# Attention inner loop: two units' value products after four score pairs, instead of one unit's after two

## The chip, the cores and the metric

The kernel runs on one core of a Trainium2 chip. The metric is device microseconds of one execution, from start to end on that core; a kernel is timed in several executions and the median counts. All times below are microseconds (us) unless marked ns.

## What is computed

The reference is one transformer layer with the norm behind each half, for one sequence of 2048 tokens, width 256, 16 heads of 16 channels, in float32:

```python
Q = X @ Wq + bq;  K = X @ Wk + bk;  V = X @ Wv + bv         # 16 heads of 16
scores = einsum('bhqd,bhkd->bhqk', q, k) / sqrt(16)
out = einsum('bhqk,bhkd->bhqd', softmax(scores), v)
out = out.transpose(0, 3, 2, 1).reshape(b, s, 256)
x = layernorm(X + out @ Wo + bo)
ffn = qmatmul(silu(qmatmul(x, w_gate)) * qmatmul(x, w_up), w_down)   # int8 weights, width 1024
x = layernorm(x + ffn)
```

## The kernel before

The kernel has three stretches: the projections of Q, K and V (up to about 47 us, with loads of keys and queries behind), the attention loop (about 53 to 541 us), and the feed-forward part (to the end). The change is in the attention loop alone.

**Units.** The loop goes over 16 steps. A step is one chunk of 512 queries for one quad of four heads (`s = u // UPS`, `UPS` = 16). A step has 16 units, one for each tile of 128 keys, so there are 256 units. Unit `u` has four heads, handled as two *score pairs* of two heads each: pair `g = 2 * u + p`, 512 pairs in all.

**Four kinds of work per unit.**
- `scores(g)` (line 1041, TensorE): two matmuls, one per head, on the two halves of the array's rows (partitions 0 and 64 on). They fill two banks of PSUM, `ps[:, 2 * ring]` and the next, with `ring = g % 3`.
- the exponential (line 556, ScalarE): one instruction over 128x1024 elements reads both banks and writes `probs[:, u % 3, 2 * p : 2 * p + 2]`. So `probs` has three slots, one for each of three units.
- `prob_times_v(u)` (line 1057, TensorE; "the value product of unit u" below): four matmuls in float32, one per head, with 17 columns of weights each (16 channels and a column of ones that gives the softmax's denominator), on four column groups of the array. They accumulate over the 16 units of a step into one PSUM bank, `ACC`. The trace shows eight matmul records for the four.
- `save_attn` (line 711, VectorE): once a step, the accumulated bank is copied out. The next step's first value product waits for it (`attn_saved`, line 1054).

**What orders them.** Each engine runs its own list of instructions in order, and semaphores join them:

```python
pe.wait_ge(exp_done, g - 2)          # line 1038, before scores(g): pair g-3 has been read
pe.wait_ge(exp_done, 2 * (u + 1))    # line 1055, before prob_times_v(u)
if p == 0 and u >= 3:                # line 553, ScalarE, before the exponential of pair 2u
    act.wait_ge(pv_done, u - 2)      # line 555: value product u-3 done, its slot is free
```

The first protects the three pairs of PSUM banks. The last protects the three slots of `probs`: the first exponential of unit `u` overwrites what the value product of unit `u-3` reads. `prob_times_v` counts up `pv_done` once, with its last matmul.

**Guests of the loop.** For three chunks, TensorE also does the output projection of the chunk before (`project_out`, line 1081, twice, in units 4 and 7 of steps 5, 9 and 13) and the transposes behind the first norm (`turn_y`, line 1095, in units 4 and 7 of steps 6, 10 and 14). They stand behind the value products of their unit.

**Loads beside the loop.** SyncE issues the loads of keys, queries and the shift rows (lines 300 to 325) from one queue. The scores of a step's first unit wait for the queries and shift rows of that step (`q_loaded`, line 1024). The shift rows of step 1 are issued behind the keys of the last quad (line 385). From step 2 on, the loads are issued a step ahead.

Of the kernel before, what the change touches and what calls it, by code (L numbers as in the profile page):

```python
# [6 lines left out]
def layer_program(nc, X, Wq, bq, Wk, bk, Wv, bv, Wo, bo, w_gate, w_up, w_down, s_gate, s_up, s_down, out):  # L7
# [36 lines left out]
    with ExitStack() as ctx:  # L44
# [842 lines left out]
        def _(pe):  # L887
# [130 lines left out]
            def scores(g):  # L1018

                u, p = g // 2, g % 2  # L1020
                s, kt, ring = u // UPS, u % UPS, g % 3
                slot = s % NSLOT
                if kt == 0 and p == 0:
                    pe.wait_ge(q_loaded[slot], loaded(s))
                    if s < QUADS:
                        pe.wait_ge(k_loaded[s], keys_of(s))
                        pe.wait_ge(ones_ready, 2 * (s + 1))
                    if s < NSLOT:
                        pe.wait_ge(bound_ready, 2 * (s + 1))
                if g == 0:  # L1030

                    pe.wait_ge(norms_ready, 2)
                elif g < 3:

                    pe.wait_ge(v_ready, 2 * (g + 1))
                else:

                    pe.wait_ge(exp_done, g - 2)
                for half in range(2):
                    base = HALF * half  # L1040
                    last = nc.tensor.matmul(ps[:, 2 * ring + half, :],  # L1041
                                            k_stack[s % QUADS][base:base + ROWS, p, kt * P:(kt + 1) * P],
                                            q_slot[slot][base:base + ROWS, p, :], start=True, stop=True)
                last.then_inc(scores_ready, 1)

            def prob_times_v(u):

                s, kt = u // UPS, u % UPS
                if u == 0:
                    pe.wait_ge(v_ones, 1)  # L1050
                    pe.wait_ge(v_ready, TT // 2)
                elif kt == 0:

                    pe.wait_ge(attn_saved, s)
                pe.wait_ge(exp_done, 2 * (u + 1))
                for hh in range(NQ):
                    last = nc.tensor.matmul(ps[32 * hh:32 * hh + VW, ACC, :],  # L1057
                                            v_all[:, kt, NQ * (s % QUADS) + hh, :],
                                            probs[:, u % 3, hh, :], start=(kt == 0), stop=(kt == TT - 1))
                last.then_inc(pv_done, 1)  # L1060

            def project_out(c, b):

                bank = FFN_BANK if c < LAST else 6 + b
                if b == 0:
                    pe.wait_ge(attn_scaled, c + 1)
                if c == 0 and b == 0:
                    pe.wait_ge(w_loaded[3], 16)
                if b == 0 and c == LAST:

                    pe.wait_ge(down_free, 2)
                if b == 0 and c:

                    pe.wait_ge(yt_ready, KO * c)
                if b == 1 and c < LAST:

                    pe.wait_ge(ln1_sum, 2 * c + 1)
                for half in range(2):
                    j = 2 * b + half
                    for ko in range(KO):  # L1080
                        last = nc.tensor.matmul(ps[:, bank, half * HID:(half + 1) * HID],  # L1081
                                                at32[:, ko, CH * j:CH * (j + 1), :].rearrange("p d u -> p (d u)"),
                                                wo[:, ko, :], start=(ko == 0), stop=(ko == KO - 1))
                last.then_inc(wo_psum, 1)

            def turn_y(c, ko):

                bank = FFN_BANK if c < LAST else 6 + ko
                if ko == 0:
                    pe.wait_ge(ln1_ready, TPC * (c + 1))  # L1090
                elif c < LAST:

                    pe.wait_ge(yt_ready, KO * c + 1)
                for j in range(TPC):
                    last = nc.tensor.transpose(ps[:, bank, j * P:(j + 1) * P], x_by[:, j, c, ko * P:(ko + 1) * P],
                                               ident[:])
                last.then_inc(yt_psum, 1)
# [3 lines left out]
            for u in range(UNITS):  # L1101
                scores(2 * u)
                scores(2 * u + 1)
                if u >= 2:
                    prob_times_v(u - 2)
                s, kt = u // UPS, u % UPS
                c = s // QUADS - 1
                if c >= 0 and s % QUADS == 1 and kt in (4, 7):
                    project_out(c, kt // 7)
                if c >= 0 and s % QUADS == 2 and kt in (4, 7):  # L1110
                    turn_y(c, kt // 7)
# [71 lines left out]
```

## Time and profile before

| what | value |
|---|---|
| time, median of 3 runs | 660.39 us (659.87 to 661.35) |
| time of the profiled execution | 661.55 us |
| its span, first to last instruction | 659.8 us |
| mean granted TensorE clock | 0.974 |
| TensorE matmuls busy | 625.1 us (95%) |
| ScalarE busy | 533.1 us (81%) |
| VectorE busy | 158.6 us (24%) |
| GpSimd busy | 69.0 us (10%) |

The profile is that of one execution. Busy time of an engine is the union of its records. Ends of matmuls are modelled, and ScalarE's record of an instruction begins before the one ahead of it has ended, so neither engine's busy share alone tells which of them sets the pace. "PE" is TensorE's matmuls, "PEld" its weight loads, "ACT" ScalarE, "DVE" VectorE, "SPq" SyncE's issuing of DMAs. A row of the timeline merges neighbouring instructions of one group: x8 is eight of them.

### The profile page before, as it was taken

The numbers are of one execution on the slowest core, as the hardware profiler recorded it, in microseconds if no ns is written. First come the engines' busy times: TensorE is split into PE (matmuls) and PEld (weight loads), VectorE is DVE, ScalarE is ACT, GpSimd is POOL, SyncE is SP. The second block draws the span as 40 slices with busy tenths as digits, with TensorE's granted clock in tenths as the row PEclk, the third lists the DMA queues.
The fourth block names the chain that finished last, engine by engine and source line by source line (L and its number), as shares of the span: only waits on it lengthen the run. The fifth ranks groups of instructions, "written<-read, shape, count | busy, mean of one in ns | idle before, by whom it ended". The sixth has DMA issues, their size and how long they took to land.

```text
span 659.8 us, 9645 instructions
## 1 busy us (share of the span) xinstructions
PE 625.1 (95%) x3938; PEld 262.0 (40%) x3938; DVE 158.6 (24%) x280; ACT 533.1 (81%) x613; POOL 69.0 (10%) x53
## 2 busy tenths in 40 slices
PE   7997969999999999999999999999999997979994
PEld 6882212222222323222232322223322235958874
DVE  6684000000001201000021200001510004695684
ACT  4526969999999899999989999999999974233351
POOL 6658600000000000000000000000400000010001
PEclk9996979999999999999999999999999997999997
DMA  9577930101112010101210110111010001010111
GB/s 215 106 107 114 128 57 8 29 6 31 18 20 60 10 26 10 28 7 30 49 24 13 22 25 10 29 41 30 6 31 3 9 2 41 1 33 0 33 33 32
DMA packets 36032, 24.40 MB, mean 37 GB/s; under 512 B 24792, under 2 KB 30808, under 8 KB 35408
## 3 DMA queue, kind: packets, MB, share of 16 engines
q1 hardware_dynamic: 34302, 23.14, 20.3%
q10 hardware_dynamic: 1682, 0.60, 0.4%
q8 instruction: 33, 0.54, 0.3%
q14 instruction: 15, 0.12, 0.1%
HBM read 6.56 MB, written 4.33 MB: 17 GB/s over the span
## 4 chain that ended last, share of the span: by engine, by line
PE 82%; SPq 7%; DVE 6%; ACT 2%; issue 1%; ACTq 1%; DMA 1%; DVEq 0%
PE ps L1057 36%; PE ps L1041 30%; PE ps L1153 5%; PE ps L1132 5%; SPq L311 4%; PE ps L920 3%; PE ps L1081 2%; SPq L313 2%; DVE h L829 1%; DVE h_lo L817 1%; ACTq L565 1%; PE ps L906 1%; DMA x_tok<-in_L_attn_X 1%; DVE stats L793 1%; SPq L300 1%
## 5 line engine op out<-in xcount | busy, mean ns | idle before, releaser
L556 ACT ACTIVATE probs<-ps 128x1024 f32<-128x1024 f32 x512 | 470.5, 1386 | 32.4 <-PE ps L1041 32.4
L1057 PE MATMUL ps<-probs,v_all 128*17 128x512 f32 x2048 | 271.8, 603 | 0.6 <-ACT probs L556 0.4
L1041 PE MATMUL ps<-q_slot,k_stack 51*128 51x512 f32 x1024 | 228.7, 492 | 11.2 <-DMA q_slot<-shift 5.7
L1041 PEld LDWEIGHTS ps<-q_slot,k_stack 51*128 51x128 f32 x1024 | 94.1, 186 | 271.4 <-ACT probs L556 245.1
L711 DVE COPY attn_q<-ps 128x512 f32<-128x512 f32 x16 | 11.1, 692 | 376.2 <-PE ps L1057 376.2
L581 ACT ACTIVATE sg<-ps,sgate_c 128x512 f32<-128x512 f32 x32 | 21.9, 688 | 61.5 <-PE ps L1153 55.5
L1057 PEld LDWEIGHTS ps<-probs,v_all 128*17 128x17 f32 x2048 | 34.1, 95 | 70.2 <-issue 63.9
L475 POOL TENSOR_TENSOR rstd<-var_eps,minus_half 128x4 f32<-128x4 f32 x4 | 4.1, 1022 | 488.9 <-DVE var_eps L743 488.9
L1153 PE MATMUL ps<-qy,wg 128*128 128x512 f32 x128 | 38.5, 425 | 9.1 <-DVE h L829 9.0
L1153 PE MATMUL ps<-qy,wu 128*128 128x512 f32 x128 | 36.1, 406 | 0.0
L1153 PEld LDWEIGHTS ps<-qy,wg 128*128 128x128 f32 x128 | 24.0, 199 | 18.8 <-DVE h L829 13.4
L1132 PE MATMUL ps<-wd,h_hi 128*128 128x256 f32 x128 | 30.9, 283 | 0.0
L1132 PE MATMUL ps<-wd,h_lo 128*128 128x256 f32 x128 | 30.9, 283 | 0.0
L829 DVE SCALAR_TENSOR_TENSOR h<-ps,sup_c,sg 128x512 f32<-128x512 f32 x32 | 23.9, 748 | 23.6 <-ACT sg L581 23.3
L436 POOL MEMSET k_stack<- 3x4096 f32 x8 | 29.1, 3637 | 3.4 <-DMA k_stack<-k_part 2.8
L1153 PEld LDWEIGHTS ps<-qy,wu 128*128 128x128 f32 x128 | 25.3, 198 | 5.9
L1132 PEld LDWEIGHTS ps<-wd,h_hi 128*128 128x128 f32 x128 | 24.7, 193 | 0.2
L1132 PEld LDWEIGHTS ps<-wd,h_lo 128*128 128x128 f32 x128 | 24.6, 192 | 0.2
L574 ACT CAST h_hi<-h 128x512 fp32r<-128x512 f32 x32 | 19.6, 613 | 3.0 <-DVE h L829 3.0
L817 DVE TENSOR_TENSOR h_lo<-h,h_hi 128x512 fp32r<-128x512 f32 x32 | 21.9, 683 | 0.4
L1081 PE MATMUL ps<-wo,at 128*128 128x256 f32 x64 | 15.6, 389 | 0.0
L1081 PEld LDWEIGHTS ps<-wo,at 128*128 128x128 f32 x64 | 11.7, 189 | 6.5 <-issue 5.1
(88 smaller groups left out, 279.1 us busy)
## 6 DMA issues: line engine op xcount, KB each, us to landing
q_slot<-qy SPq DMA_DIRECT2D x64, 64.0 KB
k_stack<-k_part SPq DMA_DIRECT2D x12, 256.0 KB, 6.3
at<-at_dram SPq DMA_DIRECT2D x8, 272.0 KB, 2.8
at_dram<-attn_q SPq DMA_DIRECT2D x62, 34.0 KB
x_tok<-in_L_attn_X SPq DMA_DIRECT2D x16, 128.0 KB, 5.3
q_slot<-qy SPq DMA_DIRECT2D x64, 32.0 KB
k_stack<-k_part SPq DMA_DIRECT2D x12, 128.0 KB, 5.1
out<-out_tmp SPq DMA_DIRECT2D x12, 128.0 KB, 2.2
```

The source lines that it names most:

```text
L311: sp.dma_start(dst[base:base + 2 * HD, hh // 2, first:last], src[row:row + HD, 0:2, first:last]).then_inc(k_loaded[quad], 16)
L436: nc.gpsimd.memset(k_stack[quad].bitcast(f32)[HALF * half:HALF * half + PROD, :, :], 1.0).then_inc(ones_ready, 1)
L556: nc.scalar.activation(probs[:, u % 3, 2 * p:2 * p + 2, :].rearrange("p a b -> p (a b)"), ps[:, 2 * ring:2 * ring + 2, :].rearrange("p a b ...
L581: nc.scalar.activation(sg[:, u % 2, :], ps[:, u % 2, :], ACT.Silu, scale=sgate_c[:, u % MT:u % MT + 1]).then_inc(silu_done, 1)
L817: nc.vector.tensor_tensor(h_lo[:, u % MT, :], h32[:, u % 2, :], h_hi[:, u % MT, :].bitcast(f32), ALU.subtract).then_inc(h_ready, 1)
L829: nc.vector.scalar_tensor_tensor(h32[:, u % 2, :], ps[:, 2 + u % 2, :], sup_c[:, m:m + 1], sg[:, u % 2, :], ALU.mult, ALU.mult).then_inc(g ...
L920: last = nc.tensor.matmul(dst, w(ko), x(ko), start=(n == 0), stop=(n == len(terms) - 1))
L1041: last = nc.tensor.matmul(ps[:, 2 * ring + half, :], k_stack[s % QUADS][base:base + ROWS, p, kt * P:(kt + 1) * P], q_slot[slot][base:base ...
L1057: last = nc.tensor.matmul(ps[32 * hh:32 * hh + VW, ACC, :], v_all[:, kt, NQ * (s % QUADS) + hh, :], probs[:, u % 3, hh, :], start=(kt == 0 ...
L1081: last = nc.tensor.matmul(ps[:, bank, half * HID:(half + 1) * HID], at32[:, ko, CH * j:CH * (j + 1), :].rearrange("p d u -> p (d u)"), wo[ ...
L1132: last = nc.tensor.matmul(ps[:, 4 + i, 0:HID], h[:, m, i * P:(i + 1) * P], wd[:, m, :], start=(m == 0 and j == 0), stop=(m == MT - 1 and j ...
L1153: last = nc.tensor.matmul(ps[:, bank, :], w[:, ko, m * P:(m + 1) * P], qy[:, c, ko, part, :], start=(ko == 0 and part == 0), stop=(ko == K ...
```

## The change

The loop on TensorE runs the value products of two units in every second iteration. With `u` odd and at least 3, the order becomes scores of pairs 2u-2 and 2u-1 (the iteration before), scores of pairs 2u and 2u+1, then the value products of units u-3 and u-2. The last two value products, of units 254 and 255, stay behind the loop as before. No semaphore, wait count or buffer changes, and no other engine's list.

```diff
             for u in range(UNITS):
                 scores(2 * u)
                 scores(2 * u + 1)
-                if u >= 2:
+                if u >= 3 and u % 2:
+                    prob_times_v(u - 3)
                     prob_times_v(u - 2)
                 s, kt = u // UPS, u % UPS
                 c = s // QUADS - 1
                 if c >= 0 and s % QUADS == 1 and kt in (4, 7):
                     project_out(c, kt // 7)
                 if c >= 0 and s % QUADS == 2 and kt in (4, 7):
                     turn_y(c, kt // 7)
             prob_times_v(UNITS - 2)
             prob_times_v(UNITS - 1)
```

## Rows read from the trace of the kernel before

**Rows 1.** The page: span and busy time of each engine.

```profile
span 659.8 us, 9645 instructions
PE 625.1 (95%) x3938; PEld 262.0 (40%) x3938; DVE 158.6 (24%) x280; ACT 533.1 (81%) x613; POOL 69.0 (10%) x53
```

**Rows 2.** Groups by line, 150 to 500 us: busy, mean ns | idle before, releaser.

```profile
L556 ACT ACTIVATE probs<-ps 128x1024 f32<-128x1024 f32 x375 | 345.1, 1409 | 7.3 <-PE ps L1041 7.3
L1057 PE MATMUL ps<-probs,v_all 128*17 128x512 f32 x1496 | 196.8, 598 | 0.0
```

**Rows 3.** Timeline, 87 to 100 us: start, length, what [idle before, releaser].

```profile
89.48 1.22 PE L1041 MATMUL ps<-q_slot,k_stack 51*128 51x512 f32 x4 [5.72 <-DMA q_slot<-shift]
...
90.32 1.94 ACT L556 ACTIVATE probs<-ps 128x1024 f32<-128x1024 f32 x2 [5.34 <-PE ps L1041]
...
93.31 7.44 ACT L556 ACTIVATE probs<-ps 128x1024 f32<-128x1024 f32 x8 [1.05 <-PE ps L1041]
...
97.03 1.05 PE L1057 MATMUL ps<-probs,v_all 128*17 128x512 f32 x8
...
98.01 0.73 PE L1041 MATMUL ps<-q_slot,k_stack 51*128 51x512 f32 x4
...
98.68 1.05 PE L1057 MATMUL ps<-probs,v_all 128*17 128x512 f32 x8
```

**Rows 4.** Timeline of ScalarE alone around 318 us, three narrow looks.

```profile
316.25 2.56 ACT L556 ACTIVATE probs<-ps 128x1024 f32<-128x1024 f32 x2
...
317.15 2.58 ACT L556 ACTIVATE probs<-ps 128x1024 f32<-128x1024 f32 x2
...
318.98 1.67 ACT L556 ACTIVATE probs<-ps 128x1024 f32<-128x1024 f32 x1
```

**Rows 5.** Timeline of weight loads alone, 320 to 322 us.

```profile
320.28 0.19 PEld L1041 LDWEIGHTS ps<-q_slot,k_stack 51*128 51x128 f32 x2 [0.85 <-ACT probs L556]
320.70 0.19 PEld L1041 LDWEIGHTS ps<-q_slot,k_stack 51*128 51x128 f32 x2 [0.24 <-ACT probs L556]
321.14 0.13 PEld L1057 LDWEIGHTS ps<-probs,v_all 128*17 128x17 f32 x8 [0.25 <-issue]
```

**Rows 6.** Timeline, 300 to 308 us, with one copy by VectorE.

```profile
300.97 1.05 PE L1057 MATMUL ps<-probs,v_all 128*17 128x512 f32 x8
...
302.09 0.69 DVE L711 COPY attn_q<-ps 128x512 f32<-128x512 f32 x1 [28.65 <-PE ps L1057]
```

**Rows 7.** Timeline, 535 to 541 us: the end of the loop.

```profile
534.27 5.27 ACT L556 ACTIVATE probs<-ps 128x1024 f32<-128x1024 f32 x5
...
537.28 1.91 PE L1057 MATMUL ps<-probs,v_all 128*17 128x512 f32 x16
...
539.60 1.05 PE L1057 MATMUL ps<-probs,v_all 128*17 128x512 f32 x8 [0.41 <-ACT probs L556]
```

**Rows 8.** Timeline, 209 to 226 us: an output projection inside the loop.

```profile
216.80 1.99 PE L1081 MATMUL ps<-wo,at 128*128 128x256 f32 x8
218.72 0.30 PEld L1041 LDWEIGHTS ps<-q_slot,k_stack 51*128 51x128 f32 x4 [0.33 <-issue]
...
219.27 5.61 ACT L556 ACTIVATE probs<-ps 128x1024 f32<-128x1024 f32 x6 [1.19 <-PE ps L1041]
```

**Rows 9.** Timeline of TensorE alone, 250 to 261 us: transposes inside the loop.

```profile
254.31 0.65 PE L1095 MATMUL ps<-ident,x_tok 128*128 128x128 f32 x4
254.89 0.73 PE L1041 MATMUL ps<-q_slot,k_stack 51*128 51x512 f32 x4
```

**Rows 10.** Timeline, 52 to 64 us: the start of the loop.

```profile
53.78 5.61 ACT L556 ACTIVATE probs<-ps 128x1024 f32<-128x1024 f32 x6 [17.12 <-PE ps L1041]
...
56.69 0.29 PEld L1041 LDWEIGHTS ps<-q_slot,k_stack 51*128 51x128 f32 x2 [0.63 <-ACT probs L556]
...
57.41 1.91 PE L1057 MATMUL ps<-probs,v_all 128*17 128x512 f32 x8
...
62.23 0.39 PEld L1041 LDWEIGHTS ps<-q_slot,k_stack 51*128 51x128 f32 x4 [1.69 <-ACT probs L556]
...
62.87 1.94 ACT L556 ACTIVATE probs<-ps 128x1024 f32<-128x1024 f32 x2 [0.85 <-PE ps L1041]
```

**Rows 11.** Timeline, 62 to 92 us: the exponentials of step 0, and SyncE's shift loads.

```profile
61.01 1.02 ACT L556 ACTIVATE probs<-ps 128x1024 f32<-128x1024 f32 x1
...
62.87 22.11 ACT L556 ACTIVATE probs<-ps 128x1024 f32<-128x1024 f32 x24 [0.85 <-PE ps L1041]
...
85.80 2.54 SPq L325 DMA_DIRECT2D q_slot<-shift  x4
```

**Rows 12.** Busy time by stretch: PE, PEld, DVE, ACT, POOL, granted clock, DMA share, GB/s.

```profile
56.00:58.00 2.00, 1.88 (x8) 0.50 (x12) 0.29 (x1) 2.00 (x3) 0.00 (x0) 0.50 0.41 85
84.00:86.00 2.00, 0.00 (x0) 0.00 (x0) 0.00 (x0) 0.98 (x2) 0.00 (x0) 1.00 0.78 102
88.00:90.00 2.00, 0.52 (x2) 0.50 (x4) 0.00 (x0) 0.00 (x0) 0.00 (x0) 0.50 0.16 26
580.00:584.00 4.00, 3.01 (x14) 2.05 (x14) 4.00 (x14) 1.60 (x3) 0.95 (x1) 1.00 0.00 0
584.00:588.00 4.00, 3.47 (x18) 2.53 (x17) 3.97 (x10) 2.27 (x4) 1.01 (x1) 1.00 0.11 23
588.00:592.00 4.00, 2.21 (x9) 1.48 (x8) 3.84 (x7) 1.54 (x3) 0.00 (x0) 0.94 0.45 112
```

## The prediction, made before the changed kernel ran

> **What bounds the kernel now.** I read the page first. Over the whole span TensorE is 95% busy and ScalarE 81% [rows 1], which points at TensorE. But both records overlap themselves, so the page can't decide, and the loop has to be read by itself.
>
> The groups by line from 150 to 500 us show 375 exponentials with 345.1 us busy of 350, and only 7.3 us in which ScalarE sat idle [rows 2]. The timeline then gives both engines' own pace. Behind the stall at step 1, TensorE catches up: one value product starts at 97.03, the next at 98.68, so a unit takes TensorE 1.65 us when nothing holds it back. In the same place ScalarE does eight exponentials in 7.44 us [rows 3]. An exponential that starts on an idle ScalarE takes 1.02 us [rows 11], and two take 1.94, so each further one takes 0.92; 1.02 + 7 x 0.917 = 7.44. ScalarE's ends in the steady loop are 316.25 + 2.56 = 318.81, 317.15 + 2.58 = 319.73 and 318.98 + 1.67 = 320.65 [rows 4], again 0.92 apart. So a unit costs ScalarE 2 x 0.917 = 1.83 us whether TensorE is ahead or not, and TensorE 1.65. **ScalarE sets the loop's pace, with 0.18 us of slack a unit on TensorE.** What matters of the change is whether ScalarE ever waits longer.
>
> How close TensorE follows is in the weight loads: the second pair's load starts at 320.70, and the exponential before it ends at 320.65 [rows 4, 5]. That pair had waited for its two PSUM banks, and started 0.05 us after they were read.
>
> **What the change removes.** No work goes: as many score matmuls, value products and exponentials as before. Switches between the two kinds of matmul halve. From a value product to scores takes 98.01 - 97.03 = 0.98 us. Two value products in a row end at 537.28 + 1.91 = 539.19 [rows 7]; alone, one lasts 1.05 [rows 6]; so the second starts 0.86 after the first, 0.12 sooner than scores would. Two score pairs and the switch behind them take 0.66 (98.68 - 98.01, to rounding) [rows 3], and one pair with its switch takes 321.14 - 320.70 = 0.44 [rows 5], so a pair followed by a pair costs 0.23 and the switch adds about 0.20. Per two units that is 0.12 + 0.20 = 0.32 us off TensorE's work. I cost it at nothing, because ScalarE's pace hides it: TensorE already has 0.36 us of slack per two units. If TensorE set the pace it would be worth 0.32 (first rival).
>
> The Trainium skill says in "TensorEngine Tiling (Array Packing)", Key Properties, that changing the tiling mode drains TensorE. The 0.20 us above agree. By that rule alone this change should pay, some 40 us over 127 pairs; by the pace read above it pays nothing.
>
> **What it moves, and the wait that this makes.** Before an odd unit u's first exponential, ScalarE waits for value product u-3 (line 555). Before the change that product stood behind the scores of unit u-1, far ahead. Now it stands behind the scores of pair 2u+1, in the same iteration, and these scores wait for pair 2u-2 to be read. So the chain that ends in exponential 2u starts only when exponential 2u-2 ends. Call that moment T:
>
> - T to the start of scores 2u+1: 0.05 [rows 4, 5]. At the half clock it was 62.23 - (61.01 + 1.02) = 0.20 [rows 10, 11].
> - scores 2u+1 to the start of value product u-3, with the switch: 0.43 (the 0.44 above).
> - start of the value product to the start of the engine that waits for it: 302.09 - 300.97 = 1.12, of which 1.05 is the product [rows 6]. That is VectorE; the trace has no exponential that waits for a value product. For ScalarE behind scores the delay is 219.27 - 218.72 = 0.55 for a pair [rows 8], so the signal itself costs little there too. Lower bound 0.98 (the product's own spacing), upper 1.19.
>
> Exponential 2u starts at T + 0.05 + 0.43 + 1.12 = T + 1.60. Exponential 2u-1, the only one ready meanwhile, is done at T + 0.917. **ScalarE stands idle for 0.68 us.** Started from idle, exponential 2u takes 1.02 in place of 0.917, which adds 0.10.
>
> What is queued behind it: exponentials 2u+1, 2u+2 and 2u+3. ScalarE ends 2u at T + 2.62, 2u+1 at 3.54, 2u+2 at 4.45, and that is the next T. Are their scores there? TensorE ends the product pair at T + 0.48 + 0.86 + 0.98 = T + 2.32, and scores 2u+2 are ready 0.55 later, T + 2.87, before 3.54. Scores 2u+3 start at 2.67, when exponential 2u has ended. So no second wait, and value product u-2 lies in the shadow. A pair of units takes 4.45 us, against 4 x 0.917 = 3.67: **+0.785 us per pair of units**. TensorE can't get ahead of this, since its scores wait for the same exponentials: the cost recurs each time.
>
> Bounds of a pair: 0.05 + 0.43 + 0.98 - 0.917 = 0.54 without a restart cost, and 0.21 + 0.43 + 1.19 - 0.917 + 0.10 = 1.01. I take 0.785, whose every term has a row of the full clock.
>
> **Step 0 is free.** At 83 us the loop before runs into the shift rows of step 1: SyncE issues them at 85.80 to 88.34 [rows 11], and the scores start at 89.48, after 5.72 us of waiting; its exponential starts at 90.32 [rows 3]. SyncE comes there whatever TensorE's pace. In the changed kernel the first part goes: exponentials 0 to 5 as before, from 53.78. The pair before the first product is 7, which waits for exponential 4, done at 53.78 + 1.02 + 4 x 0.917 = 58.47. At the half clock the steps are 0.13, 0.72 (57.41 - 56.69) and 1.91 + 0.07 [rows 10], so exponential 6 starts at 61.3 and 9 ends at 65.07. Before, it ended at 62.87 + 1.94 = 64.81: 0.26 later only. The other 22 exponentials of step 0 take 20.17, with six waits (u = 5 to 15) 4.71, which ends them at 89.95. Scores of step 1 start at 89.48 as before, at the full clock since TensorE has not stood idle, so exponential 32 starts at 90.03, 33 ends at 91.97, and 34, with a wait of its own, starts at 91.05 + 1.60 = 92.65. Before, 34 started at 93.31 [rows 3]. The changed kernel is **0.66 us ahead** there.
>
> **The rest.** Odd units 19 to 255 are 119, so 119 x 0.785 = 93.4.
>
> Output projections: before, each took 218.72 - 216.80 = 1.92 of TensorE and cost ScalarE 1.19 idle and 0.10 of restart [rows 8], six times: 7.7. In the changed order, one in unit 4 ends at T - 1.35 + 1.92 = T + 0.57; two pairs of scores (0.66) follow, and the value product starts at T + 1.23 in place of 0.48: +0.75. One in unit 7 stands behind the product pair, so scores 2u+2 are ready at T + 2.32 + 1.92 + 0.55 = 4.79 against 3.54: +1.25 and 0.10 of restart. Three times each: 6.3, which is 1.4 less. Transposes take 0.58 (254.89 - 254.31) [rows 9] and fit in both places: unit 4 ends at T - 0.77, and unit 7 makes scores ready at T + 3.45. Nothing before, nothing now.
>
> The wait for `attn_saved` goes nowhere: the copy of the last bank (0.69) ends at about T + 3.2, and the next step's first product starts at T + 4.93. Loads from step 2 on are issued a step ahead. The end is unchanged: the last exponential ends, and product 255 starts 0.06 later (534.27 + 5.27 = 539.54, then 539.60) [rows 7]; all that follows hangs on that.
>
> **Sum.** 93.4 - 0.66 - 1.4 = +91.4 us. The profiled execution took 661.55 us, 1.75 more than its span and 1.2 more than the median; by its own time the changed kernel takes 661.55 + 91.4 = 752.9, and set on the median, 660.39 + 91.4 = 751.8. I say 752.
>
> **Rivals.**
> - *TensorE sets the pace* (faster). Place: the steady loop. If TensorE's matmuls were the limit, the 0.32 us saved per two units would come off: 240 units in the steady loop make 120 x 0.32 = 38 us, 622 us. It decides once an exponential takes less than half of TensorE's 1.65, that is 0.82. For it speaks the 95% of the page; against it the constant 0.917 while TensorE catches up. 2%.
> - *The wait is hidden* (no change). The third slot of `probs` would have to cover it, which needs T + 1.60 to be before T + 0.917; a remaining wait under 0.03 us per pair would be within the measurement, and one below about 0.015 would be outweighed by the 2.1 us gained elsewhere. Only a different order of events than the waits in the code would do that. 1%.
> - *ScalarE waits for the whole product pair*, if the second product's matmuls hold up the end of the first: they fill the same four column groups. Then the chain is 0.86 longer: 0.86 x 119 = +102 and 0.86 x 6 = +5 in step 0, about 859 us. Against it: a product alone and the first of two have the same spacing within 0.12. 4%.
> - *TensorE's clock falls.* TensorE would now idle about a quarter of the time, in gaps of about 0.5 us. The granted clock was at its lower level (1.2 GHz, 0.50) in 56 to 58 us, at the loop's start, and in 88 to 90 us, behind the 5.72 us in which TensorE stood still [rows 3]. With 3.47 of 4 and 3.01 of 4 us busy in small gaps it stayed at 1.00, and in 588 to 592 (2.21 busy) it was still 0.94 [rows 12]. At the lower level the chain is 0.20 + 0.72 + 1.98 = 2.90, and a pair of units 2.90 + 1.02 + 2 x 0.917 = 5.75, +2.09: some 910 us if it held throughout, about 785 if a fifth of the time. 5%.
>
> The Trainium skill, in "TensorE: Matmul & The Clock Gate", section "A second HAM failure mode: psum-queue depth-cycling", tells of a kernel whose short idle moments between groups of matmuls made the clock swing between both levels. By that rule the last rival would come true; no row here shows it for gaps this short.
>
> **Numbers.** The forecast itself has 88%. The range goes by the bounds of the pair: 119 x 0.54 = 64 less 2.1 gives 722, and 119 x 1.01 = 120 less 2.1 gives 778. No other case reaches in from below, and a clock that falls for part of the time does from above. Both ends need all terms off the same way, so I cut the lower to 727 and leave 780 above. A change of 0.2% (1.3 us) is about what a measurement of this kernel can tell from none. Slower: 88 + 4 + 5 = 97%; same 1%; faster 2%.
>
> **What the profile after would show.** The exponentials idle about 0.68 us before every fourth, released by the value products of line 1057, some 125 times and about 85 us in all; in unit pairs of 4.45 us. Value products come as x16 with 1.91 us, the second 0.86 behind the first. PE's busy share falls to about 85% with the clock still near 0.97. No wait of several us for the shift rows near 84 us, and the loop ends near 631. The forecast is wrong if these waits are absent, if they are near 1.5 us each (the whole pair), or if matmuls of the loop show a clock of 0.50. If only a term is off, it should be the 1.12 from product to exponential, the only one taken from another engine.

## The result, and the profile after

The changed kernel takes 759.68 us in the median of four runs, and the kernel before took 660.69 beside it: a ratio of 1.15, 95% interval 1.148 to 1.152. That is 99 us slower. The prediction said 752, with 727 to 780 as its range.

The page of the changed kernel, first the span and busy times, then the chain of work that ended last, then two groups by line (busy, mean ns | idle before, releaser):

```profile
span 758.8 us, 9645 instructions
PE 630.8 (83%) x3938; PEld 275.8 (36%) x3938; DVE 158.6 (21%) x280; ACT 545.9 (72%) x613; POOL 69.0 (9%) x53
...
ACT 45%; PE 42%; DVE 6%; issue 4%; ACTq 1%; DMA 1%; SPq 0%; DVEq 0%
...
L556 ACT ACTIVATE probs<-ps 128x1024 f32<-128x1024 f32 x512 | 483.3, 1029 | 119.4 <-PE ps L1057 98.6
L1041 PE MATMUL ps<-q_slot,k_stack 51*128 51x512 f32 x1024 | 244.2, 497 | 104.8 <-ACT probs L556 98.9
```

TensorE does the same 3938 matmuls in nearly the same time (630.8 us, 625.1 before); what grew by 99 us is the span. The new wait has a name: the exponentials stand idle 98.6 us until a value product (line 1057) has ended. The groups before, [rows 2], show no such releaser. TensorE in its turn waits 98.9 us for exponentials: each engine waits for the other, within one pair of units.

ScalarE's timeline of the changed kernel, in steps 4 and 5:

```profile
215.41 3.77 ACT L556 ACTIVATE probs<-ps 128x1024 f32<-128x1024 f32 x4 [0.74 <-PE ps L1057]
219.93 3.77 ACT L556 ACTIVATE probs<-ps 128x1024 f32<-128x1024 f32 x4 [0.75 <-PE ps L1057]
...
247.80 2.85 ACT L556 ACTIVATE probs<-ps 128x1024 f32<-128x1024 f32 x3 [1.50 <-PE ps L1057]
```

Four exponentials, then a hole of 0.75 us, every 4.52 us. Without the hole and its restart four exponentials take 3.67 [rows 3, 4]. In the last row an output projection (unit 4 of step 5) stands ahead of the hole, and the hole is 0.75 longer.

Both engines around one hole:

```profile
299.71 2.85 ACT L556 ACTIVATE probs<-ps 128x1024 f32<-128x1024 f32 x3
...
301.70 0.50 PE L1041 MATMUL ps<-q_slot,k_stack 51*128 51x512 f32 x2 [0.41 <-ACT probs L556]
...
302.13 1.91 PE L1057 MATMUL ps<-probs,v_all 128*17 128x512 f32 x16
...
303.31 3.77 ACT L556 ACTIVATE probs<-ps 128x1024 f32<-128x1024 f32 x4 [0.75 <-PE ps L1057]
```

ScalarE ends exponential 2u-1 at 299.71 + 2.85 = 302.56, so 2u-2 ended at 301.64. The scores start at 301.70 (0.06 later), the product 0.43 behind them, and exponential 2u 1.18 behind the product. It starts at 303.31, while TensorE is still at the second product (the pair lasts to 304.04). So ScalarE waits for the first product alone.

Where the shift rows of step 1 land:

```profile
89.55 0.74 PE L1041 MATMUL ps<-q_slot,k_stack 51*128 51x512 f32 x4 [0.17 <-DMA q_slot<-shift]
...
93.17 3.77 ACT L556 ACTIVATE probs<-ps 128x1024 f32<-128x1024 f32 x4 [0.75 <-PE ps L1057]
```

Where TensorE stood still for 5.72 us before [rows 3], it waits 0.17. Exponential 34 starts at 93.17, against 93.31 before.

### The profile page after: what moved, and what is told of

Its sections match the earlier page's. It is cut to its first block, busy times and chain, and to the rows that moved or that the text cites. A ratio compares the mean times of both kernels' runs of the same rounds, so it can differ in the third digit from the quotient of the medians.

```text
span 758.8 us, 9645 instructions
## 1 busy us (share of the span) xinstructions
PE 630.8 (83%) x3938; PEld 275.8 (36%) x3938; DVE 158.6 (21%) x280; ACT 545.9 (72%) x613; POOL 69.0 (9%) x53
## 4 chain that ended last, share of the span: by engine, by line
ACT 45%; PE 42%; DVE 6%; issue 4%; ACTq 1%; DMA 1%; SPq 0%; DVEq 0%
ACT probs L556 44%; PE ps L1057 19%; PE ps L1041 9%; PE ps L1154 4%; PE ps L1133 4%; PE ps L920 3%; PE ps L1081 2%; DVE h L829 1%; DVE q_slot L672 1%; DVE h_lo L817 1%; ACTq L565 1%; PE ps L906 1%; DMA x_tok<-in_L_attn_X 1%; DVE v_all L651 1%; DVE stats L793 0%
## 5 line engine op out<-in xcount | busy, mean ns | idle before, releaser
L556 ACT ACTIVATE probs<-ps 128x1024 f32<-128x1024 f32 x512 | 483.3, 1029 | 119.4 <-PE ps L1057 98.6
L1041 PE MATMUL ps<-q_slot,k_stack 51*128 51x512 f32 x1024 | 244.2, 497 | 104.8 <-ACT probs L556 98.9
L1057 PE MATMUL ps<-probs,v_all 128*17 128x512 f32 x2048 | 246.1, 598 | 0.4 <-ACT probs L556 0.4
L1057 PEld LDWEIGHTS ps<-probs,v_all 128*17 128x17 f32 x2048 | 47.1, 97 | 113.3 <-issue 71.8
L727 DVE TENSOR_TENSOR x_tok<-x_tok,ps 128x512 f32<-128x512 f32 x8 | 5.5, 688 | 40.0 <-PE ps L1081 40.0
```

The lines of the kernel that those rows point to most:

```text
L556: nc.scalar.activation(probs[:, u % 3, 2 * p:2 * p + 2, :].rearrange("p a b -> p (a b)"), ps[:, 2 * ring:2 * ring + 2, :].rearrange("p a b ...
L1041: last = nc.tensor.matmul(ps[:, 2 * ring + half, :], k_stack[s % QUADS][base:base + ROWS, p, kt * P:(kt + 1) * P], q_slot[slot][base:base ...
L1057: last = nc.tensor.matmul(ps[32 * hh:32 * hh + VW, ACC, :], v_all[:, kt, NQ * (s % QUADS) + hh, :], probs[:, u % 3, hh, :], start=(kt == 0 ...
```

## The experiments

Seven theories are in play: the slot wait (mine); the pairing as such; a gain from fewer switches; a wait for the whole pair; TensorE's clock; TensorE as the pace; and a second limit in the three pairs of PSUM banks, first named in the expectations of pair_sooner and four_slots. Every kernel's loop is shown against the changed one unless said otherwise, and ratios are to the kernel before, run beside it.

### The lag without the pairing: single_late

Against the kernel before:

```diff
-                if u >= 2:
-                    prob_times_v(u - 2)
+                if u >= 3:
+                    prob_times_v(u - 3)
...
+            prob_times_v(UNITS - 3)
             prob_times_v(UNITS - 2)
```

> No pairing: one value product behind every two score pairs, as before the change, but of unit u-3 in place of u-2. My theory: the lag alone makes the wait, and now in every unit: exponential 2u starts at T + 0.06 + 0.43 + 1.18 = T + 1.67 in place of T + 0.917, and 0.10 of restart, so a unit takes 2.69 us in place of 1.83: +0.85 x 239 = 204, and some 6 more in step 0: about 870 us, far above the changed kernel. Rival (pairing is the cause): about 660.

Measured: 1109.66 us, ratio 1.679 (1.663 to 1.695). The direction is as expected and says that a product one unit later is enough for the wait, without any pairing. The size is far off. ScalarE's and TensorE's timeline, and busy time by stretch (PE, PEld, DVE, ACT, POOL, granted clock, DMA share, GB/s):

```profile
95.60 1.94 ACT L556 ACTIVATE probs<-ps 128x1024 f32<-128x1024 f32 x2 [1.90 <-PE ps L1057]
96.68 0.80 PE L1041 MATMUL ps<-q_slot,k_stack 51*128 51x512 f32 x2 [0.48 <-ACT probs L556]
...
97.41 1.91 PE L1057 MATMUL ps<-probs,v_all 128*17 128x512 f32 x8
...
99.44 1.94 ACT L556 ACTIVATE probs<-ps 128x1024 f32<-128x1024 f32 x2 [1.90 <-PE ps L1057]
...
90.00:130.00 40.00, 35.18 (x130) 7.32 (x122) 0.69 (x1) 19.39 (x20) 0.00 (x0) 0.50 0.08 13
```

A unit takes 99.44 - 95.60 = 3.84 us, and the granted clock is 0.50: one value product lasts 1.91 in place of 1.05. The chain at this clock is 0.06 + 0.73 + 2.03 + 1.02 = 3.84.

At first the clock did not fall: it did not rise. Both this kernel and the changed one enter the loop at 0.50. The same stretch of single_late and of the changed kernel:

```profile
64.00:68.00 4.00, 3.52 (x16) 0.73 (x12) 0.00 (x0) 1.94 (x2) 1.19 (x1) 0.50 0.92 141
64.00:68.00 4.00, 3.18 (x22) 0.93 (x22) 0.00 (x0) 3.25 (x5) 1.61 (x1) 1.00 0.85 119
```

single_late stays at 0.50 up to its first output projection near 370 us. Behind the projections it is at 1.00 for a while, and then falls back, with nothing but units of its own loop in between:

```profile
395.00:400.00 5.00, 3.57 (x24) 0.82 (x22) 0.00 (x0) 3.50 (x5) 0.00 (x0) 1.00 0.00 0
...
397.43 0.51 PE L1041 MATMUL ps<-q_slot,k_stack 51*128 51x512 f32 x2 [0.77 <-ACT probs L556]
...
400.73 1.91 PE L1057 MATMUL ps<-probs,v_all 128*17 128x512 f32 x8
...
400.00:405.00 5.00, 4.40 (x18) 1.06 (x22) 0.00 (x0) 2.92 (x4) 0.00 (x0) 0.53 0.00 2
```

In that stretch at 1.00 a unit took the 2.69 us worked out, and TensorE waited 0.77 once a unit. So the new wait both keeps the clock from rising and lets it fall, and the slower products make the wait longer. (With the waits filled, in single_late_busy below, the clock is at 1.00 in 64 to 68 us.)

### The signal behind the whole pair: late_signal

```diff
-                    prob_times_v(u - 3)
-                    prob_times_v(u - 2)
+                    prob_times_v(u - 3, 0)      # counts pv_done up by 0
+                    prob_times_v(u - 2, 2)      # by 2, with its last matmul
```

> The changed kernel, but the pair of value products counts pv_done up by two with its last matmul, in place of one with each product's last. My theory: the exponential now waits for the whole pair, 0.86 us longer, 119 times from step 1 on and about 5 in step 0: +107, about 866 us, with idle of 1.61 us before every fourth exponential in place of 0.75. Rival (in the changed kernel the exponential already waits for more than the first product): unchanged at 760.

Measured: 1024.03 us, ratio 1.549 (1.536 to 1.562). The changed kernel therefore waits for the first product only. Again the size is off by the clock. A pair of units, and a stretch:

```profile
97.67 3.77 ACT L556 ACTIVATE probs<-ps 128x1024 f32<-128x1024 f32 x4 [3.06 <-PE ps L1057]
...
101.30 3.06 PE L1057 MATMUL ps<-probs,v_all 128*17 128x512 f32 x16
...
104.50 3.77 ACT L556 ACTIVATE probs<-ps 128x1024 f32<-128x1024 f32 x4 [3.06 <-PE ps L1057]
...
130.00:170.00 40.00, 30.26 (x144) 7.85 (x140) 0.69 (x1) 22.63 (x24) 0.00 (x0) 0.76 0.07 11
```

The product pair lasts 3.06 us in place of 1.91, since most of it runs at the lower level, and the mean clock is 0.76. It falls and comes back within the pair of units of 6.83 us: 0.88 from 96 to 99.5 us and 0.61 from 99.5 to 103.

### TensorE kept busy: single_late_busy and late_signal_busy

Each is the kernel above, with score matmuls repeated into the same banks:

```diff
-                for half in range(2):
+                for half in [0, 1] * (1 + again(g)):
...
+            def again(g):      # single_late_busy
+                return 4 if g % 2 == 0 and g >= 8 else 0
+            def again(g):      # late_signal_busy
+                return (4, 2, 2, 0)[g % 4] if g >= 8 else 0
```

> The single late value products took 1110 us, not the 870 worked out at the full clock, and their trace shows a granted clock of 0.50 in most of the loop. This kernel is the same with TensorE's idle time filled: each unit's first pair of score matmuls is issued five times over into the same two banks (4 x 0.21 = 0.85 us more of matmuls a unit, with the same result), in time in which TensorE waits anyway. If the clock fell because TensorE stood idle too much, it stays at 1.00, a unit takes the 2.69 us worked out before, and the kernel some 870 us, 240 less for more matmuls. If the clock fell for another reason, or the wait is longer for another, it stays near 1110 or gets slower.

> The late signal took 1024 us, not 866, with a granted clock that swings between 1.00 and 0.50 every few us. This kernel is the same with TensorE's idle time filled by repeated score matmuls (8 x 0.21 = 1.7 us more of matmuls per pair of units, with the same result). If idling lowered the clock, it stays at 1.00, a pair of units takes 4.53 + 0.86 = 5.39 us, and the kernel 866 us. Otherwise near 1024 or more.

Measured: 875.45 us (ratio 1.322, 1.318 to 1.326) and 874.22 us (1.320, 1.316 to 1.324). More matmuls made the first kernel 234 us faster and the second 150. From single_late_busy's timeline, and the same stretch of time in both kernels:

```profile
302.52 1.94 ACT L556 ACTIVATE probs<-ps 128x1024 f32<-128x1024 f32 x2 [0.75 <-PE ps L1061]
...
305.21 1.94 ACT L556 ACTIVATE probs<-ps 128x1024 f32<-128x1024 f32 x2 [0.75 <-PE ps L1061]
...
300.00:340.00 40.00, 40.00 (x304) 18.13 (x302) 3.46 (x5) 28.54 (x30) 0.00 (x0) 1.00 0.09 15
```

```profile
303.86 3.77 ACT L556 ACTIVATE probs<-ps 128x1024 f32<-128x1024 f32 x4 [1.61 <-PE ps L1061]
...
300.00:340.00 40.00, 40.00 (x306) 18.66 (x306) 3.46 (x5) 28.41 (x31) 0.00 (x0) 1.00 0.09 15
```

A unit takes 2.69 us, the hole is 0.75 in every unit, and the clock stays at 1.00. With the whole pair to wait for it is 1.61, which is 0.86 more, as worked out. So the two sums for the holes were right at the full clock, and TensorE's idling was what had lowered it. Why the totals are 5 and 8 us above the sums was not taken apart.

### The slot freed in three ways, products still in pairs

pair_sooner runs the pair of units u-2 and u-1 behind the scores of an even u:

```diff
-                if u >= 3 and u % 2:
-                    prob_times_v(u - 3)
+                if u >= 2 and u % 2 == 0:
                     prob_times_v(u - 2)
+                    prob_times_v(u - 1)
```

> The value products stay in pairs, but one unit sooner: units u-2 and u-1 behind the scores of an even u, so that every exponential's slot of probs is free long before. My theory (the loss is the wait for a slot, made by the lag and not by the pairing): that wait goes. What is left is the next limit, the three pairs of PSUM banks: from the end of an exponential 0.06 + 0.43 + 1.84 + 0.55 = 2.88 until the next scores are ready, against 3 x 0.917 = 2.75 of work that ScalarE has in hand, so 0.13 and 0.10 of restart per pair of units, 120 times, +28 us: about 688 us, with idle of about 0.13 us before an exponential released by the scores and none by the value products. Rival (the pairing itself costs, whatever its place: the second product holds up the first): stays near 760. Rival (the pairing saves time once the slot wait is gone): at or below 660.

four_slots keeps the changed order. A fourth slot lies, from unit 16 on, in memory that the keys' source no longer needs:

```diff
-                if p == 0 and u >= 3:
+                if p == 0 and 3 <= u < UPS:
                     act.wait_ge(pv_done, u - 2)
...
+                if p == 0 and u > UPS:
+                    act.wait_ge(pv_done, u - 3)
...
-                    probs[:, u % 3, 2 * p:2 * p + 2, :].rearrange("p a b -> p (a b)"),
+                    slot_of(u)[:, 2 * p:2 * p + 2, :].rearrange("p a b -> p (a b)"),
```

> The changed order as it is, with a fourth slot of probs from step 1 on (unit 16), so that an exponential waits for the value product of four units before. My theory: the slot wait is what costs; from step 1 on it goes and the same rest of 0.23 us per pair of units is left by the PSUM banks: about 689 us. Rival (the order costs through TensorE, by its switches, its clock or its weight loads): stays near 760. Rival (no second limit): about 661.

pair_between puts the pair ahead of the second score pair:

```diff
                 scores(2 * u)
-                scores(2 * u + 1)
                 if u >= 3 and u % 2:
                     prob_times_v(u - 3)
                     prob_times_v(u - 2)
+                scores(2 * u + 1)
```

> The pair of value products u-3 and u-2 stands between the two score pairs of an odd u, in place of behind them. My theory: the product now starts from the exponential before (0.917 earlier), so its slot is free at T + 0.75, before ScalarE asks for it at T + 0.917; the second score pair is late instead, ready at T - 0.917 + 0.06 + 0.43 + 1.84 + 0.55 = T + 1.96 against 1.83: again 0.13 + 0.10 per pair of units, about 688 us. Rival (only the slot wait and no PSUM limit): 661. Rival (pairing costs in itself): 760.

Measured: 693.64 us (ratio 1.050, 1.044 to 1.057), 689.24 us (1.044, 1.037 to 1.051) and 684.38 us (1.036, 1.033 to 1.038), for 688, 689 and 688 expected. Three different ways to free the slot take away 66 to 75 of the 99 us, and none comes back to the kernel before. Pairing alone neither costs 99 us nor saves any. The steady loop of pair_between, then of four_slots:

```profile
233.38 118.39 ACT L556 ACTIVATE probs<-ps 128x1024 f32<-128x1024 f32 x122 [1.33 <-PE ps L1041]
```

```profile
98.67 1.94 ACT L570 ACTIVATE probs_more<-ps 128x1024 f32<-128x1024 f32 x2
...
106.45 1.94 ACT L570 ACTIVATE probs_more<-ps 128x1024 f32<-128x1024 f32 x2
```

A pair of units takes 4 x 118.39 / 122 = 3.88 us in the one and (106.45 - 98.67) / 2 = 3.89 in the other, against 3.67. The 122 exponentials in 118.39 us are 0.970 apart, not 0.917, though no hole is long enough to be listed. This is the second limit. Let an exponential end and free its pair of banks for the last scores ahead of a product pair. From there ScalarE has three exponentials to do, 2.75 us, and the scores behind the product pair are ready only after 2.88. pair_sooner's timeline, with two narrow looks at single exponentials, shows the whole loop:

```profile
299.47 1.91 PE L1057 MATMUL ps<-probs,v_all 128*17 128x512 f32 x16
...
300.69 1.05 ACT L556 ACTIVATE probs<-ps 128x1024 f32<-128x1024 f32 x1
...
301.31 0.97 PE L1041 MATMUL ps<-q_slot,k_stack 51*128 51x512 f32 x6
...
301.85 1.02 ACT L556 ACTIVATE probs<-ps 128x1024 f32<-128x1024 f32 x1
...
302.93 0.50 PE L1041 MATMUL ps<-q_slot,k_stack 51*128 51x512 f32 x2 [0.64 <-ACT probs L556]
...
303.36 1.91 PE L1057 MATMUL ps<-probs,v_all 128*17 128x512 f32 x16
```

One exponential ends at 301.74, and the next starts at 301.85, 0.54 behind the scores that follow the product pair. It ends at 302.87, and the last scores ahead of the next product pair, which had waited 0.64 for it, start 0.06 later. The only wait of scores for an exponential inside a step is that for their banks (line 1038). The loop is 0.06 + 0.43 + 1.84 + 0.54 + 1.02 = 3.89. A fourth pair of banks was not tried: beside these six banks the kernel uses bank 6 for the value products and bank 7 for the guests.

The 9 us between pair_sooner and pair_between (6.9 between the profiled executions) lie at the guests and at step 1. In pair_sooner's ScalarE timeline, behind an output projection and behind transposes that follow a product pair:

```profile
230.07 5.82 ACT L556 ACTIVATE probs<-ps 128x1024 f32<-128x1024 f32 x6 [2.04 <-PE ps L1041]
...
262.97 93.18 ACT L556 ACTIVATE probs<-ps 128x1024 f32<-128x1024 f32 x96 [0.71 <-PE ps L1041]
```

A guest behind a product pair finds nothing left in ScalarE's stock, so even transposes cost there (0.71 of idling), which were free before.

### The pair taken apart: split

```diff
                 scores(2 * u)
+                if u >= 3 and u % 2:
+                    prob_times_v(u - 3)
                 scores(2 * u + 1)
                 if u >= 3 and u % 2:
-                    prob_times_v(u - 3)
                     prob_times_v(u - 2)
```

> In an odd u: scores 2u, value product u-3, scores 2u+1, value product u-2. The two products are no longer next to each other, with the same lags as the changed kernel. My theory: the first product is in time for its slot (T + 0.75) and no group of matmuls is longer than a product and a pair of scores, so ScalarE sets the pace again: 655 to 662 us (step 1's stall remains). Rival (the lag of three units costs whatever the place): above 700.

Measured: 665.03 us, ratio 1.006 (1.0036 to 1.0084). Each product still runs in the same iteration as in the changed kernel; only value product u-3 and scores 2u+1 have changed places, and 95 of the 99 us are back. It is 3 us above what was expected. Its ScalarE timeline:

```profile
97.63 123.14 ACT L556 ACTIVATE probs<-ps 128x1024 f32<-128x1024 f32 x134 [1.14 <-PE ps L1041]
222.35 5.61 ACT L556 ACTIVATE probs<-ps 128x1024 f32<-128x1024 f32 x6 [1.57 <-PE ps L1057]
229.62 23.94 ACT L556 ACTIVATE probs<-ps 128x1024 f32<-128x1024 f32 x26 [1.67 <-PE ps L1041]
253.81 5.61 ACT L556 ACTIVATE probs<-ps 128x1024 f32<-128x1024 f32 x6 [0.25 <-PE ps L1057]
259.76 82.60 ACT L556 ACTIVATE probs<-ps 128x1024 f32<-128x1024 f32 x90 [0.34 <-PE ps L1041]
```

The steady loop is at 0.917 again (134 in 123.14). What is left, 7.7 us at the end of the loop in this execution (667.65 us), sits in three places of about 2.4 us each. The output projections leave 1.57 and 1.67 of idling, against 1.19 and 1.25 in the kernel before, the first now released by a value product. The transposes leave 0.25 and 0.34 and two restarts, where they had cost nothing. And exponential 36, at step 1, starts at 97.63, against 95.24 before, of which 1.5 is there when the step begins (91.78 against 90.32). The slot is free in time in the steady loop, but with little to spare (0.17 us by the expectation).

### Short exponentials: before_short and sooner_short

```diff
-                    probs[:, u % 3, 2 * p:2 * p + 2, :].rearrange("p a b -> p (a b)"),
-                    ps[:, 2 * ring:2 * ring + 2, :].rearrange("p a b -> p (a b)"),
+                    probs[:, u % 3, 2 * p, :],
+                    ps[:, 2 * ring, :],
...
-                                            probs[:, u % 3, hh, :], start=(kt == 0), stop=(kt == TT - 1))
+                                            probs[:, u % 3, 2 * (hh // 2), :], start=(kt == 0), stop=(kt == TT - 1))
```

> The order before the change, with every exponential halved: it covers only the first head of its pair, and the value products read that head's values for both (so the second head's exponential is left out). ScalarE then needs about 0.52 us in place of 0.917 and TensorE sets the pace: 1.65 us per unit, 256 units, 0.18 x 240 = 43 us less: about 615 us. If ScalarE's 0.917 was not the pace but something else in the chain, it stays at 660.

> The same halved exponentials (the second head's left out) with the value products in pairs one unit sooner. By the rule that fewer switches of tiling pay, the pairs of units take 2.96 us in place of 3.29: 40 us less than the short kernel in the order before. My theory: three pairs of PSUM banks don't allow it: from the end of an exponential 2.88 us until the next scores are ready, and 0.62 for that exponential from idle, 3.50 per pair of units against 3.29: about 25 us more than the short kernel in the order before, about 640 us.

Measured: 628.16 us (ratio 0.950, 0.947 to 0.952) and 643.03 us (0.972, 0.969 to 0.975). First the order before, then the pairs:

```profile
302.33 1.05 PE L1057 MATMUL ps<-probs,v_all 128*17 128x512 f32 x8
...
303.98 1.05 PE L1057 MATMUL ps<-probs,v_all 128*17 128x512 f32 x8
```

```profile
301.94 1.91 PE L1057 MATMUL ps<-probs,v_all 128*17 128x512 f32 x16
...
305.40 1.91 PE L1057 MATMUL ps<-probs,v_all 128*17 128x512 f32 x16
```

These kernels leave out half of the exponentials' work. That makes the loop faster, down to TensorE's 1.65 us per unit: ScalarE had been the pace. The 628 is 13 above what I expected. Some 7 us of it are the guests, which the sum left out: with TensorE as the limit they cost their full time, 6 x (1.92 + 0.58) = 15.0 us, where they had cost 7.3 of idling and 0.6 of restarts. The rest was not taken apart. In pairs, with fewer switches, two units take 3.46 us against 3.30: even with short exponentials the 0.32 saved doesn't show, since the PSUM banks run out first (3.50 worked out).

### The guests in pieces: guests_split

Against the kernel before, `project_out` is issued one matmul (of its eight) per unit:

```diff
-                if c >= 0 and s % QUADS == 1 and kt in (4, 7):
-                    project_out(c, kt // 7)
+                if c >= 0 and s % QUADS == 1 and (4 <= kt < 8 or 9 <= kt < 13):
+                    project_piece(c, kt - 4 if kt < 8 else kt - 5)
```

> The order before the change, but the output projections inside the loop are cut into eight pieces of one matmul pair each (0.24 to 0.48 us) in eight units of their step, in place of two blocks of 1.92 us in two units. In the kernel before, each block left ScalarE idle for 1.19 us and cost 0.10 of restart, so the three PSUM pairs took up 1.92 - 1.29 = 0.63 us of it, and the transposes (0.58) cost nothing. My theory (ScalarE sets the pace and only groups of matmuls longer than its stock of scores cost): pieces of 0.24 to 0.48 us cost nothing, 6 x 1.29 = 7.7 us less, about 653 us. Rival (TensorE sets the pace, so that its work costs wherever it stands): 660 or more.

Measured: 661.28 us, ratio 0.9991 (0.9972 to 1.0009): no difference, and the expectation was wrong. The timeline shows why:

```profile
218.65 0.70 PE L1074 MATMUL ps<-wo,at 128*128 128x256 f32 x2
219.28 0.73 PE L1041 MATMUL ps<-q_slot,k_stack 51*128 51x512 f32 x4
219.82 1.94 ACT L556 ACTIVATE probs<-ps 128x1024 f32<-128x1024 f32 x2 [0.33 <-PE ps L1041]
...
222.09 1.94 ACT L556 ACTIVATE probs<-ps 128x1024 f32<-128x1024 f32 x2 [0.33 <-PE ps L1041]
```

One piece takes 0.63 us up to the next scores, not 0.24 to 0.48; eight of them take 5.0 where two blocks took 3.84. A unit with a piece takes 2.27 on TensorE against ScalarE's 1.83. The first is absorbed, and each one after it shows as 0.33 of idling. By these numbers (0.44 too much per piece, 0.18 to spare per unit) one piece in every three or four units would be free; that is an estimate.

## Why the prediction was right, and where it was off

**ScalarE sets the pace: right.** before_short is the direct test.

**The new wait, its place and its releaser: right.** 127 holes released by line 1057, 98.6 us in all (the prediction said some 125 and about 85). That it comes from the place of value product u-3, and not from the pairing, is shown by single_late, which has the wait without pairs, and by pair_sooner, four_slots and pair_between, which have pairs and no such wait in the steady loop. split narrows it down: the lag of three units alone costs nothing in the steady loop, as long as the product stands ahead of scores 2u+1. Behind them it hangs on exponential 2u-2, as the prediction's chain has it.

**The size per pair of units: 0.853 in place of 0.785.** The mis-sized term is the one marked as the doubtful one, from product to waiting exponential: 1.18 for ScalarE, where the copy on VectorE [rows 6] had given 1.12. The first term was 0.06, not 0.05. Together 0.07 a pair, times 119 is 8.1 us; with the 0.5 of step 0 below, 91.4 + 8.1 + 0.5 = 100.0. The last value product starts 99.8 later (639.44 against 539.60), and the part behind the loop took 0.8 less in this execution. Restart (0.10), the 0.43 and the second product in the shadow stood.

**Step 0: right in kind.** The stall at the shift rows was absorbed; the changed kernel was 0.14 us ahead at exponential 34, not 0.66. Its loop began 0.22 later (54.00 against 53.78), and each of the six waits was 0.07 longer, so that exponential 32 no longer waited for the shift rows at all.

**Guests: right.** The hole at a projection in unit 4 grew by 0.75, as worked out, and the three in unit 7 left 1.2 us each, where 1.25 was worked out.

**Rivals.** A wait for the whole pair is ruled out by the trace and by late_signal. A gain from fewer switches: 0.12 of it is there (the pair in 1.91), and it never reached the time, with short exponentials either. The rule of the Trainium skill ("TensorEngine Tiling (Array Packing)", Key Properties) that a change of tiling mode drains the engine fits the 0.20 us of the rows. It could not decide the time: the stock of scores bounds how long a group of matmuls may be.

**The clock** was not at fault in the changed kernel, and the rival was real all the same. Its trace has 1.00 in the loop with TensorE's records covering 83% of it:

```profile
150.00:500.00 350.00, 290.17 (x1886) 92.02 (x1890) 25.16 (x52) 288.19 (x307) 2.08 (x2) 1.00 0.11 19
```

A wait only 0.86 us longer per pair of units was enough for the clock to fall. This is where my expectations of two runs failed, by 240 and 158 us, and the busy variants show the clock as the cause. The prediction also put TensorE's idling at a quarter of the loop; the records leave 17%. That the changed kernel stayed clear of it is in part luck: the prediction gave the falling clock 5% and had no row with gaps this short, and 0.86 us more of waiting per pair of units did put late_signal at 1024.

**Open.** How much more waiting the changed kernel would have stood before its clock fell. No version beat the kernel before: split and guests_split come within a per cent.

## What to carry to other kernels

Before regrouping matmuls, write down from which earlier event each buffer comes free, and follow that chain through both engines at the new place: here moving a product behind one more pair of scores cost 0.85 us per pair of units though no work was added, and exchanging two lines gave nearly all of it back. A longer group on one engine needs a longer stock for the other: three pairs of banks hold 2.75 us, and a chain of 2.88 through the product pair to the next scores already costs. If a new wait makes TensorE idle, work out the time at both levels of its clock.

## What the runs showed that was not expected

Short, regular waits can lower TensorE's clock, and can hold it at the lower level from the start. At the full clock TensorE waited 0.77 us once per unit of 2.69 us in single_late, and the clock fell; in the changed kernel it waited 0.41 twice per pair of units of 4.52 and kept 1.00. At the lower clock single_late's waits were only 0.48, since the slower matmuls fill more of the time, and still the clock stayed at 0.50 for hundreds of microseconds. Filling the waits with repeated matmuls brought 1110 us down to 875.

The section "A second HAM failure mode: psum-queue depth-cycling" of "TensorE: Matmul & The Clock Gate" in the Trainium skill tells of a clock that swings between its two levels with short idle moments between groups of matmuls. late_signal's trace agrees, with 0.76 on average.
